# Decoder on one core: two gathered sums behind three quads, 28 of 64 sums moved into the second attention

## The chip, the cores and the metric

The kernel runs on one core of one Trainium2 chip, all in float32. The metric is the device time of one execution in microseconds (us). TensorE (PE) multiplies, VectorE (DVE) and ScalarE (ACT) work elementwise, GpSimd (POOL) issues the gathers and scatters, SyncE (SP) issues the plain transfers; 16 DMA engines carry them.

## What is computed

A decoder of two layers on x of 4 sequences by 1024 tokens by 256. After each block the residual is added and a layer norm taken:

```python
x = _layernorm(x + _L0_attn_ref(x, ...))    # retention, 8 heads
x = _layernorm(x + _L0_xattn_ref(x, ctx))   # 16 heads against 77 context rows
x = _layernorm(x + _L0_ffn_ref(x, ...))     # 64 experts, top 8 of them, and 2 shared experts
x = _layernorm(x + _L1_attn_ref(x, ...))    # linear attention with a memory
x = _layernorm(x + _L1_xattn_ref(x, ctx))
x = _layernorm(x + _L1_ffn_ref(x, ...))     # 8 gated experts, top 2
```

The change is in the third line and where it runs into the fourth. The first feed-forward is, for each token, `sum over its 8 experts of cw[e] * (silu(x @ W1[e] + B1[e]) @ W2[e] + B2[e])`, plus two shared experts of hidden width 512.

## The kernel before

The program has four phases, each a set of five instruction streams (one an engine): attention 1 (`attention_phase`, layer 0), the first feed-forward (`feed_phase`), attention 2 (the same function, layer 1) and the second feed-forward (`gated_phase`). A phase waits in `begin_here` for the last transfers of the one before. Tokens go in 8 steps of 4 x 128.

**Feed-forward.** Attention 1 has scattered each token's row into 8 places of a list in HBM (`lists`), sorted by expert in pages of 128 rows. The phase takes them in 80 quads of four pages. For quad n SyncE loads 512 KB (`load_quad`), TensorE transposes them (line 1680), multiplies them by the first weights (1692) and by the second (1703), ScalarE copies and applies silu (1551, 1575), and SyncE stores 512 KB to `results`. VectorE copies the weights of quad n+1 into place, four of the first kind (1597) and four of the second (1602), a quad ahead of TensorE. Between the quads lie the units of the shared experts (lines 110 and 127: 8 a step), the weights of the tokens, and the sums.

**Weights.** "weigh" jobs on VectorE, six a step, turn two tables of a step into the 8 weights of each token: compare, multiply, reduce (1648, 1652, 1654) for two pairs of sequences. SyncE loads the tables of a step into `routed` (`load_route`, 1493); only the compare and the multiply read them.

**Sums.** There are 64, one for each step s and eighth k (number n = 8s + k). For sum n GpSimd issues four gathers of 128 rows each from `results` (`gather`, line 1405), a small operation before them (`rest`, line 158), into one of four buffers; it needs the sum four numbers back to be done. VectorE adds the rows, times their weights, to the step's accumulator (`add_up`, line 1420, four instructions). Some gathers carry more work:
- k = 0 waits for the stores of all quads that can hold the step's rows (24 + 8s of them);
- k = 1 issues the accumulator's load (`load_base`, line 1387);
- k = 4 computes the scale of the norm of step s-1 (`scale`, lines 1375 and 1377), after that step's statistics;
- k = 7 issues the store of step s-1 (`store`, line 1381), and waits for its norm.

VectorE takes the statistics (1429, 1435) with sum k = 7 and the norm of step s-1 (`norm`, line 1441) behind sum k = 4 of step s. There are two accumulators.

**Where they lie.** `feed_order` writes out the order of the jobs: the first 24 quads have two units in three; from quad 24 on (`begun`) every other quad has a unit, and from quad 26 on each has one sum, as long as sums are left; those up to `LATE` - 1 (40 of 64) stay in the phase. Units end at quad 65. Each engine follows this order. GpSimd, which has only gathers here, issues `LATE + AHEAD` groups in a row.

**Late sums.** The other 24 are called from attention 2 by `late_on_pool` (gather of n + 3) and `late_on_vector` (sum n, and the norm if n % 8 is 4). Three stand ahead of its loop, behind `begin_here` and some memsets; 21 and the last norm hang on jobs of the loop, which `with_late` lists.

**Attention 2's order.** `SEQUENCE1` lists jobs with a lead; in loop step t a job with lead a works on step t - a of the tokens. Each engine takes its part of each job in this order. Of one loop step: wout and its norm (ln2 for the second norm), q (query), rank, four mx (maximum of the scores, line 830, GpSimd not involved), sig, tri, num, up (state), sc (scores, exponential on ScalarE, line 645), pv, wo, ln1 (the first norm), put (scatters, line 592). For ln1 and ln2 VectorE takes statistics, GpSimd computes the scale (lines 540 to 543) and ScalarE applies it (656 for ln1, 664 for ln2):

```python
    ("x1t", 2, 0), ("x1t", 2, 1), ("wout", 3, 0), ("wout", 3, 1), ("q", 2, 0), ("rank", 4, 0), ("q", 2, 1),
    ("ln2", 3, 0), ("put", 4, 0), ("lqk", 1, 0), ("mx", 2, 0), ("lv", 1, 0), ("sig", 1, 0), ("x2t", 3, 0),
    ...
    ("sc", 2, 2), ("ln1", 1, 0), ("pv", 2, 1), ("sc", 2, 3), ("pv", 2, 2), ("pv", 2, 3),
```

The waits that order late work on GpSimd against VectorE:

```python
            if s >= 1 and k == 7:
                store(pool, s - 1)
            ...
            if c >= NG:
                pool.wait_ge(summed, c - NG + 1)
```

## Time and profile before

| | |
|---|---|
| median of 3 runs | 2044.65 us (2043.0 to 2046.52) |
| the profiled execution | 2043.22 us, span 2041.2 us |
| TensorE busy | 1712.8 us (84%), mean granted clock 0.911 |
| VectorE busy | 1168.8 us (57%) |
| GpSimd busy | 922.9 us (45%) |
| ScalarE busy | 628.1 us (31%) |
| first feed-forward, quads | 640 to 1124 us |
| attention 2 | 1128 to 1600 us |
| second feed-forward | 1600 to 2041 us |

A row of a timeline gives start and duration in us, engine, line, operation, the output and inputs by their names, and in brackets how long the engine had been idle and what released it. `big` is one large buffer: the first weights, the gather buffers and the accumulators lie in it. In the windows a clock of 1.00 is TensorE's full speed, and the DMA share is the mean busy share of the 16 engines.

### The profile page before, as it was taken

The numbers are of one execution on the slowest core, as the hardware profiler recorded it, in microseconds if no ns is written. First come the engines' busy times: TensorE is split into PE (matmuls) and PEld (weight loads), VectorE is DVE, ScalarE is ACT, GpSimd is POOL, SyncE is SP. The second block draws the span as 40 slices with busy tenths as digits, with TensorE's granted clock in tenths as the row PEclk, the third lists the DMA queues.
The fourth block names the chain that finished last, engine by engine and source line by source line (L and its number), as shares of the span: only waits on it lengthen the run. The fifth ranks groups of instructions, "written<-read, shape, count | busy, mean of one in ns | idle before, by whom it ended". The sixth has DMA issues, their size and how long they took to land.

```text
span 2041.2 us, 49463 instructions
## 1 busy us (share of the span) xinstructions
PE 1712.8 (84%) x19787; PEld 1385.2 (68%) x19787; DVE 1168.8 (57%) x3042; ACT 628.1 (31%) x957; POOL 922.9 (45%) x1020
## 2 busy tenths in 40 slices
PE   3899999987859999777788449989997499999994
PEld 2677777776536776555566327777775399999993
DVE  3467777775302545667554537876765245665564
ACT  0233333332212555434446113434433011111110
POOL 0016777888850004888882576542322201222223
PEclk9999999998879999889989668878988699999997
DMA  9415665575693777878878633223101512333332
GB/s 307 154 36 182 203 205 180 180 256 187 180 247 104 230 218 250 265 251 260 259 253 280 226 91 96 72 70 135 44 33 37 180 48 71 94 93 92 98 96 62
DMA packets 269648, 322.85 MB, mean 158 GB/s; under 512 B 25083, under 2 KB 245487, under 8 KB 268655
## 3 DMA queue, kind: packets, MB, share of 16 engines
q1 hardware_dynamic: 236399, 227.38, 35.2%
q0 software_dynamic: 33024, 92.32, 14.1%
q8 instruction: 160, 2.62, 0.5%
q14 instruction: 65, 0.53, 0.1%
HBM read 157.22 MB, written 162.40 MB: 157 GB/s over the span
## 4 chain that ended last, share of the span: by engine, by line
PE 58%; POOL 14%; DVE 8%; DMA 6%; issue 6%; ACT 5%; SPq 2%; DVEq 0%; POOLq 0%; ACTq 0%
PE wide L2031 13%; POOL big L1405 7%; PE d_yp L2043 6%; ACT pt L645 3%; PE bank L994 3%; PE wide L1160 3%; PE wide L110 3%; PE wide L127 2%; POOL rest_ones L158 2%; PE bank L1175 2%; PE bank L1183 2%; PE wide L1163 2%; PE e_yp L1703 2%; PE wide L1147 2%; PE wide L1692 2%
## 5 line engine op out<-in xcount | busy, mean ns | idle before, releaser
L1405 POOL DMA_INDIRECT big<-results,slots x256 | 263.0, 1027 | 266.5 <-DMA results<-e_y 190.5
L2031 PE MATMUL wide<-d_xt,d_ws 128*128 128x128 f32 x2272 | 278.7, 277 | 0.6 <-issue 0.6
L2031 PEld LDWEIGHTS wide<-d_xt,d_ws 128*128 128x128 f32 x2272 | 272.3, 193 | 4.5 <-issue 1.0
L583 POOL DMA_INDIRECT lists<-big,slots x160 | 158.8, 993 | 82.3 <-issue 37.8
L645 ACT ACTIVATE pt<-wide 77x2048 f32<-77x2048 f32 x64 | 119.9, 1873 | 164.8 <-PE wide L1163 161.9
L1420 DVE SCALAR_TENSOR_TENSOR big<-big,weights 128x256 f32<-128x256 f32 x256 | 107.2, 480 | 83.5 <-DMA big<-results,slots 72.8
L1692 PE MATMUL wide<-e_xt,e_w1s 128*64 128x128 f32 x1280 | 96.1, 297 | 65.5 <-DVE e_w1s L1597 65.5
L127 PE MATMUL wide<-shared_sw,shared_sh 128*128 128x256 f32 x512 | 125.8, 390 | 25.6 <-DVE big L1661 25.6
L127 PEld LDWEIGHTS wide<-shared_sw,shared_sh 128*128 128x128 f32 x512 | 99.7, 196 | 69.0 <-DVE big L1661 29.4
L1900 POOL DMA_INDIRECT d_picked<-results,slots x64 | 63.5, 992 | 181.3 <-DMA results<-d_y 168.6
L1931 ACT ACTIVATE d_gate<-wide 128x512 f32<-128x512 f32 x71 | 42.4, 597 | 326.7 <-PE wide L2031 326.7
L2043 PE MATMUL d_yp<-d_wd,d_h 128*128 x568 | 134.2, 380 | 0.0
L158 POOL TENSOR_TENSOR rest_ones<-rest_ones 128x4 f32<-128x4 f32 x120 | 133.1, 1110 | 2.2
L110 PE MATMUL wide<-shared_sx,shared_sw 128*128 128x512 f32 x256 | 131.7, 639 | 2.5 <-ACT shared_sh L118 2.5
L837 DVE RECIPROCAL rden<-bank 128x256 f32<-128x256 f32 x64 | 112.1, 1751 | 37.6 <-PE bank L1175 36.5
L1692 PEld LDWEIGHTS wide<-e_xt,e_w1s 128*64 128x64 f32 x1280 | 75.1, 147 | 81.1 <-DVE e_w1s L1597 72.4
L2043 PEld LDWEIGHTS d_yp<-d_wd,d_h 128*128 128x128 f32 x568 | 102.8, 191 | 10.9
L540 POOL TENSOR_TENSOR rs<-mv,eps 128x4 f32<-128x4 f32 x32 | 6.6, 206 | 228.0 <-DVE mv L694 227.8
L1551 ACT ACTIVATE e_xt<-e_xp 128x1024 f32<-128x1024 f32 x80 | 81.9, 1024 | 83.5 <-PE e_xp L1680 83.5
L1962 DVE COPY d_ws<-big 128x1024 f32 x142 | 92.4, 693 | 26.4 <-issue 25.3
L1980 DVE TENSOR_TENSOR d_h<-d_gate,wide 128x512 f32<-128x512 f32 x71 | 48.7, 686 | 97.2 <-PE wide L2031 97.2
L1703 PE MATMUL e_yp<-e_w2s,e_ht 64*128 64x256 f32 x640 | 100.9, 438 | 1.5 <-ACT e_y L1551 1.5
(277 smaller groups left out, 3538.6 us busy)
## 6 DMA issues: line engine op xcount, KB each, us to landing
lists<-zero SPq DMA_DIRECT2D x20, 2048.0 KB, 14.3
e_x<-lists SPq DMA_DIRECT2D x80, 512.0 KB, 5.6
results<-e_y SPq DMA_DIRECT2D x80, 512.0 KB
d_x<-lists SPq DMA_DIRECT2D x71, 128.0 KB, 2.2
results<-d_y SPq DMA_DIRECT2D x71, 128.0 KB, 1.7
e_w<-in_L_w SPq DMA_DIRECT2D x2, 4096.0 KB, 38.9
x<-in_x SPq DMA_DIRECT2D x8, 512.0 KB, 5.0
shared_sw<-in_x_t SPq DMA_DIRECT2D x32, 128.0 KB
```

The lines of the kernel that those rows point to most:

```text
L110: ins = nc.tensor.matmul(sp_h, self.sw1[:, c, u * P:(u + 1) * P], self.sx[:, s % 2, c], start=c == 0, stop=c == KC - 1)
L127: ins = nc.tensor.matmul(sp_y[b // 2][:, b % 2 * DM:(b % 2 + 1) * DM], self.sh[:, n % 2, b * P:(b + 1) * P], self.sw2[:, u], start=u == 0 ...
L158: step(self.nc.gpsimd.tensor_tensor(self.ones[:, 1], self.ones[:, 0], self.ones[:, 0], ALU.pow))
L583: pool.indirect_dma_start(out=lists, out_offset=bass.IndirectOffsetOnAxis(ap=slots[:, b, i, k:k + 1], axis=0), in_=z2[i % 3][:, b, :], in_ ...
L645: empties(nc.scalar.activation(pt[0:CTX, p % 2].rearrange("k (j n) -> k j n", j=4), ps[0:CTX], ACT.Exp, scale=score_scale), job)
L837: step(nc.vector.reciprocal(rden[:, p % 2], ps[:, KC * P:]))
L1405: pool.indirect_dma_start(out=picked[:, c % NG, b, :], out_offset=None, in_=results[0:-(-PAGES_OF_STEP[s] // 4) * 4 * R0, :], in_offset=ba ...
L1420: ins = nc.vector.scalar_tensor_tensor(out=acc[s % NA][:, b], in0=picked[:, n % NG, b], scalar=weights[:, b, s, k:k + 1], in1=acc[s % NA][ ...
L1692: ins = mm(hp[h * H0:(h + 1) * H0, a * R0:(a + 1) * R0], w1s[:, j % NW1, h, a, c], xt[:, j % 2, h, a, c], start=c == 0, stop=c == KC - 1)
L1703: ins = mm(yp[:, h, a * DM:(a + 1) * DM], ht[lanes, j % 2, a], w2s[lanes, j % NW2, a, 0:DM], start=True, stop=True)
L2031: ins = mm(out[T % 2][:, a * P:(a + 1) * P], ws[:, T % NW, n, c, a * P:(a + 1) * P], xt[:, T % 2, c], start=c == 0, stop=c == KC - 1)
L2043: ins = mm(yp[T % 2][:, 0:DM], h[:, T % 2, c * P:(c + 1) * P], wd_flat[:, bass.ds(e * (HC * DM) + c * DM, DM)], start=c == 0, stop=c == HC ...
```

## The change

Sums lie behind two of three quads from quad 26 on, so that 36 fit by quad 79 (`LATE` goes from 40 to 36). The other 28 are late: three of them, gathers and sums, stand ahead of `begin_here` of attention 2 and its memsets, and 25 and the last norm hang on jobs of the loop, five instead of four in each of four loop steps (behind q, two mx, num and now up). With this each late number moves: the groups with k = 7 (47, 55, 63) were issued at sig 0, num 1 and num 3; now 47 is at wo 0, 55 at the last mx of loop step 3, and 63 at q of loop step 5, ahead of ln2. The load of a step's route tables is issued one job sooner, at the last weigh job of the step before.

```diff
--- before.py
+++ after.py
@@ -190,7 +190,7 @@
 
     behind = [("x0t", 0, 1), ("sig", 0, 0), ("tri", 0, 1), ("num", 0, 1), ("ct", 0, 0), ("wo", 0, 1)]
     for i in range(4):
-        behind += [("q", i, 1), ("mx", i, 1), ("mx", i, 3), ("num", i + 1, 1)]
+        behind += [("q", i, 1), ("mx", i, 1), ("mx", i, 3), ("num", i + 1, 1), ("up", i + 1, 0)]
     out = []
     for job in order:
         out.append(job)
@@ -543,6 +543,9 @@
                 nc.gpsimd.tensor_tensor(rs[:, which, 3], rs[:, which, 2], rs[:, which, 1], ALU.mult)\
                     .then_inc(rstd[which], 1)
 
+            if not first:
+                for n in range(LATE, LATE + 3):
+                    late_on_pool(pool, n)
             begin_here(pool)
             nc.gpsimd.memset(half[:], -0.5)
             nc.gpsimd.memset(minus[:], -1.0)
@@ -551,9 +554,6 @@
             if first:
                 nc.gpsimd.memset(zero[:], 0.0).then_inc(pool_ready, 1)
             pool.wait_ge(pool_ready, POOL_READY - (2 if first else 0))
-            if not first:
-                for n in range(LATE, LATE + 3):
-                    late_on_pool(pool, n)
             pool.wait_ge(consts, 16 * len(loads))
             if first:
                 for n in range(ES):
@@ -693,6 +693,9 @@
                 nc.vector.bn_aggr(mv[:, which, numbers[0]], stats[:, which, numbers[0]])
                 nc.vector.bn_aggr(mv[:, which, numbers[1]], stats[:, which, numbers[1]]).then_inc(mv_done[which], 1)
 
+            if not first:
+                for n in range(LATE, LATE + 3):
+                    late_on_vector(dve, n)
             begin_here(dve)
             if first:
                 nc.vector.memset(state[:], 0.0).then_inc(state_done, 1)
@@ -702,9 +705,6 @@
                 make(nc.vector.memset(v[:], 1.0))
             make(nc.vector.memset(vals[:], 0.0))
             make(nc.vector.memset(ones[:], 0.0))
-            if not first:
-                for n in range(LATE, LATE + 3):
-                    late_on_vector(dve, n)
             dve.wait_ge(consts, 16 * len(loads))
             make(nc.vector.tensor_reduce(mask2[:], head_mask[:].rearrange("p (m h) -> p h m", h=2), AX.X, ALU.add))
             make(nc.vector.tensor_reduce(sel_at[:], ident[:].rearrange("p (r n) -> p n r", r=4)[:, 0:4], AX.X, ALU.add))
@@ -1223,7 +1223,7 @@
 PAGES_OF_STEP = [(NB * P * K0 * (s + 1)) // R0 + E0 - 1 for s in range(STEPS)]
 
 
-LATE = STEPS * K0 - 24
+LATE = STEPS * K0 - 28
 AHEAD = 3
 FIRST_UNITS = 20
 PLAN_BEHIND = UNITS + 4
@@ -1274,7 +1274,7 @@
         else:
             weights(1)
             units(1 if j % 2 else 0)
-        if j >= begun + 2:
+        if j >= begun + 2 and (j - begun) % 3:
             sums(1)
     while unit[0] <= TOTAL:
         units(1)
@@ -1506,9 +1506,9 @@
                         load_quad(n + NX)
                     if n:
                         store_quad(n - 1)
-                if kind == "weigh" and n % 6 == 0 and n:
-                    sp.wait_ge(weighed, n - 1)
-                    load_route(n // 6)
+                if kind == "weigh" and n % 6 == 5 and n + 1 < 6 * STEPS:
+                    sp.wait_ge(weighed, n)
+                    load_route((n + 1) // 6)
                 if kind == "unit" and n and n % UNITS == 0 and shared < STEPS:
                     sp.wait_ge(experts.full, n)
                     experts.load_rows(sp, src_t, shared)
```

## Rows read from the trace of the kernel before

**Rows 1.** The page, part 4: the chain that ended last, shares of the span by engine

```profile
PE 58%; POOL 14%; DVE 8%; DMA 6%; issue 6%; ACT 5%; SPq 2%; DVEq 0%; POOLq 0%; ACTq 0%
```

**Rows 2.** Waits, 802 to 1127 us: engine line waited for, us, times, longest

```profile
DVE big L1420 <- DMA big<-results,slots: 68.7, 27, 4.6
...
PE wide L1692 <- DVE e_w1s L1597: 65.1, 21, 6.8
```

**Rows 3.** Line L1405, 788 to 1086 us: duration ns min/median/max, first and last start

```profile
L1405 POOL DMA_INDIRECT big<-results,slots x172: 942/967/2157, 788.4 to 1084.6; - x172
```

**Rows 4.** Timeline of VectorE, first feed-forward: start us, us, what, idle before

```profile
802.11 1.67 DVE L1420 SCALAR_TENSOR_TENSOR big<-big,weights 128x256 f32<-128x256 f32 x4 [5.30 <-DMA big<-mid]
...
875.70 1.22 DVE L1648 TENSOR_TENSOR big<-e_routed,e_slots_f 128x1024 f32<-128x1024 f32 x1 [4.90 <-DMA e_routed<-route]
...
1069.70 1.67 DVE L1420 SCALAR_TENSOR_TENSOR big<-big,weights 128x256 f32<-128x256 f32 x4 [1.37 <-DMA big<-results,slots]
```

**Rows 5.** Timeline of TensorE, first feed-forward

```profile
909.80 1.97 PE L1692 MATMUL wide<-e_xt,e_w1s 128*64 128x128 f32 x16 [6.49 <-DVE e_w1s L1597]
...
924.59 1.99 PE L110 MATMUL wide<-shared_sx,shared_sw 128*128 128x512 f32 x4
...
928.14 1.04 PE L1680 MATMUL e_xp<-e_ident,e_x 128*128 128x128 f32 x8
...
1095.44 1.09 PE L1680 MATMUL e_xp<-e_ident,e_x 128*128 128x128 f32 x8
...
1098.55 1.09 PE L1680 MATMUL e_xp<-e_ident,e_x 128*128 128x128 f32 x8
...
1118.41 1.09 PE L1692 MATMUL wide<-e_xt,e_w1s 128*64 128x128 f32 x16
```

**Rows 6.** Windows: us, busy us of PE, PEld, DVE, ACT, POOL, clock, DMA share, GB/s

```profile
640.00:788.00 148.00, 145.37 (x1040) 103.99 (x1039) 71.94 (x236) 80.59 (x121) 0.00 (x0) 0.98 0.69 217
...
802.00:1118.50 316.50, 248.44 (x1850) 179.06 (x1852) 196.46 (x660) 145.07 (x221) 233.20 (x222) 0.89 0.82 263
...
1085.00:1115.00 30.00, 26.18 (x268) 19.88 (x264) 13.72 (x69) 22.02 (x35) 0.60 (x1) 1.00 0.97 315
```

**Rows 7.** Timeline of GpSimd, end of the feed-forward and attention 2

```profile
1064.88 0.96 POOL L1405 DMA_INDIRECT big<-results,slots  x1 [0.30 <-issue]
...
1165.56 0.81 POOL L1381 DMA_DIRECT2D mid<-big  x1 [11.31 <-DVE big L1441]
...
1198.93 0.21 POOL L540 TENSOR_TENSOR rs<-mv,eps 128x4 f32<-128x4 f32 x1
...
1284.24 0.19 POOL L540 TENSOR_TENSOR rs<-mv,eps 128x4 f32<-128x4 f32 x1 [8.30 <-DVE mv L694]
...
1314.16 0.96 POOL L592 DMA_INDIRECT lists<-shared_sw,slots  x1 [0.30 <-issue]
...
1333.79 0.95 POOL L1405 DMA_INDIRECT big<-results,slots  x1 [0.30 <-issue]
...
1351.72 0.20 POOL L540 TENSOR_TENSOR rs<-mv,eps 128x4 f32<-128x4 f32 x1 [10.66 <-DVE mv L694]
```

**Rows 8.** Timeline of ScalarE, attention 2

```profile
1200.73 2.08 ACT L656 ACTIVATE x<-x,rs 128x256 f32<-128x256 f32 x4 [25.52 <-POOL rs L543]
...
1286.29 2.06 ACT L656 ACTIVATE x<-x,rs 128x256 f32<-128x256 f32 x4
...
1336.56 2.08 ACT L656 ACTIVATE x<-x,rs 128x256 f32<-128x256 f32 x4 [3.24 <-POOL rs L543]
```

**Rows 9.** Timeline of VectorE, attention 2

```profile
1142.88 0.16 DVE L709 TENSOR_REDUCE mask<-head_mask 128x2 f32<-128x8 f32 x1 [7.09 <-DMA memory<-in_L_norm]
...
1163.89 1.37 DVE L1441 TENSOR_SCALAR big<-big,sums_mv 128x256 f32<-128x256 f32 x4
...
1268.58 1.66 DVE L1420 SCALAR_TENSOR_TENSOR big<-big,weights 128x256 f32<-128x256 f32 x4
...
1355.82 1.67 DVE L1420 SCALAR_TENSOR_TENSOR big<-big,weights 128x256 f32<-128x256 f32 x4
```


## What it will do to the time

> **What bounds the kernel now.** I read the chain of waits first: its shares [rows 1] name TensorE 58% and GpSimd 14%, so somewhere GpSimd sets the pace. The waits of the first feed-forward say where: VectorE stands 68.7 us before its sums for gathered rows, and TensorE 65.1 us for staged expert weights [rows 2]. These are one wait seen twice. VectorE works in program order, so a sum that waits for its rows also holds back the weight copies written behind it. GpSimd itself never stops: 172 gather instructions between 788.4 and 1085.6 us [rows 3] are 43 groups of four, 6.91 us each, and each quad has one sum. So from the first sum (802.11) to the last (1069.70) [rows 4] 40 quads go at 6.9 us.
>
> TensorE would not need that. A quad alone takes 3.11 us (1095.44 to 1098.55) and a shared unit 3.55 (924.59 to 928.14) [rows 5]; with half a unit per quad that is 4.9 us. The last 14 quads have neither sum nor unit and are at the transfers' limit: 315 GB/s over 1085 to 1115 at a busy share of 0.97, while the whole stretch from 802 to 1118.5 moves 263 GB/s at 0.82 [rows 6].
>
> **Part 1: two sums behind three quads (feed-forward).** The condition drops every third sum, so 36 sums lie behind quads 26 to 79 instead of 40 behind 26 to 65. Three limits for this stretch, now 316.3 us (802.1 to 1118.4, the last inward group [rows 4, 5]):
> - GpSimd: 36 groups by 6.91 from 788.4 end at 1037; a sum starts 4.8 us after its last gather's issue (1064.88 [rows 7], 1069.70 [rows 4]) and takes 1.67: some 242 us after 802.
> - TensorE: 54 x 3.11 + 20 units x 3.55 = 239 us.
> - Transfers: 263 GB/s x 316.5 us = 83.2 MB now. Four gather groups (each four times 128 rows of 1 KB, 0.524 MB, as much as one quad's load) and one step's load and store go out of it, each as much again: 6 x 0.524 = 3.1 MB. 80.1 MB at 315 GB/s are 254 us.
>
> All three are close, so I don't take the largest as it stands. The plain quads behind 65 need 3.1 us of TensorE but about 4.7 of transfers (1.05 MB for load and store, 0.35 for gathers, 0.09 for the accumulators); the 40 before need 5.1 us of transfers against 4.9: 40 x 5.1 + 14 x 4.7 = 270, less some 6 us for loads and gathers that are ahead at the start, 264. Nothing overlaps fully; at 5% lost it is 277. **Term: -40 us**; bounds -62 (254 us reached) and -18 (298 us, each quad 0.8 us over the transfer time). I take the value nearer the transfers' row because with four buffers the gathers run ahead and VectorE stops meeting them.
>
> The Trainium skill ("DMA: Bandwidth & Descriptors", Specifications) states an HBM limit of about 358 GB/s per core. By it the bytes would need only 224 us, and the 242 us of GpSimd would bound; the stretch would shrink by over 60 us. No stretch of this length here shows more than 315.
>
> **Part 2: route rows a quad sooner.** SyncE issues the load at the sixth part of a step's weights, ahead of the next quad's waits. Its wait (five parts done) is the same number, and only the reduce, which doesn't read the rows, is still open. VectorE waited 4.90 us at 875.70 [rows 4]. Ahead of quad 24 TensorE is 98% busy regardless (145.4 of 148 us, [rows 6]); behind it the wait would eat part of term 1. I take 0 by itself; between 0 and -5. Behind SyncE's load nothing is queued that is late: one issue of half a microsecond.
>
> **Part 3: three late sums ahead of the wait for the quads.** Before, GpSimd waited for the last quad's store and issued three groups beside the constants' loads, which hide them. Now groups 39 to 41 go out while the last quads drain. What they bring lies ahead of attention 2's first norm. Now group 47, the last of a step's eight, must wait for VectorE's norm of the step before; GpSimd idles 11.31 us until 1165.56, then issues five groups, and the scale for the first norm starts at 1198.93 [rows 7]: ScalarE stands 25.52 us until 1200.73 [rows 8]. After the change groups 42 to 46 go out between 1143 (the constants' landing, at which VectorE goes on at 1142.88 [rows 9]) and about 1184: each needs the sum three late places back, and these come at 1156, 1164, 1167 and 1172, so GpSimd has three groups' work (19 us) behind 1164. Group 47 then needs the norm after "wo", about 1183: 1184 + 0.8 + 6.3 = 1191 instead of 1198.9. **Term: -7.5 us**; between -12 and 0. The transfers of these twelve gathers now share the drain with the last stores: 0 to +2, taken 0.
>
> **Part 4: 28 late sums instead of 24, five a step instead of four.** This is where the change costs. GpSimd has the gathers and the norms' scales in one queue. A group costs 6.27 us there: from the last scatter (ends 1315.12) to the last gather (ends 1334.74) are three groups and a store, 0.81 us by the one at 1165.56 [rows 7]. The groups that end a step (47, 55, 63) carry a store that waits for VectorE's norm, which is issued with the same late sum. By steps of the attention, all in today's clock:
> - Loop steps are counted from 0, as the schedule does. Step 2: the fifth group fits; GpSimd ends about when the scale's input is ready: +0.5.
> - Loop step 3: group 55 moves to the last maximum. The sum there starts at 1268.58 and takes 1.66, the norm 1.37 by the one at 1163.89 [rows 9]: 1271.6. Then store 0.8, a base load as long and three groups 18.8: 1292.1. The scale is issued at 1284.24 today with 8.30 us of idleness ahead [rows 7], and ScalarE takes it at 1286.29 without a wait [rows 8]: +7.9, and the exponential queued behind it on ScalarE, with its product on TensorE, are late by the same.
> - Loop step 4: behind the scatters (1315.12) come four groups (25.1) and a two-instruction scale, which I put at 1.2 since the four-instruction one takes 1.8 (1198.93 to 1200.73 [rows 7, 8]), where three groups and a store are now: 1341.4 against 1334.74, and ScalarE already waits 3.24 us today [rows 8]: +6.6.
> - Loop step 5: group 63 now stands ahead of the second norm's scale. VectorE's sum starts at 1355.82 [rows 9]; 1357.5 + 1.4 + 0.8 + 6.3 = 1366.0 against 1351.72 [rows 7]: 14 later. Between 0 and 4 us of it TensorE may have as slack, I allow 2: +12.
> - Four more sums on VectorE, 1.67 us each: 0 to +6.7, taken +2, since most fall where it waits for TensorE.
> - Two new idle stretches of 8 and 12 us. After 6.49 us of idleness a group of 16 matmuls took 1.97 us instead of 1.09 [rows 5], the pace of the lower of the two clock levels (1.2 against 2.4 GHz); the catch-up there cost some 3 us. 0 to +6, taken +3.
>
> **Term: 0.5 + 7.9 + 6.6 + 12 + 2 + 3 = +32 us**; bounds +10 (the waits overlap with slack I don't see) and +42.
>
> **Sum:** -40 + 0 - 7.5 + 32 = -15.5. The profiled execution took 2043.22 us with a span of 2041.2; it becomes about 2027.7. It stands 1.4 us below the median of the three runs (2044.65), within their spread, so I give **2028**.
>
> **Rivals.**
> (a) *Slower: the step-ending groups win.* Place: the GpSimd queue of the attention's loop steps 3 to 5. Price: +42 with both clock losses, no slack and all sums in full, against a feed-forward that gets only -27 as the transfers leave more gaps, and -7.5: 2043.2 + 7.5 = 2051. It decides from the point where part 4 costs more than parts 1 and 3 bring. For it: the queue order is certain. Against it: the feed-forward's wait is large and plain [rows 2].
> (b) *Much faster.* The feed-forward reaches its 254 us, -62, and the late groups cost only +20 as the scales find slack: 2043.2 - 62 - 7.5 + 20 = 1994; half-way, about 2008. For it: 315 GB/s is held for 30 us [rows 6]. Against it: only where nothing but quads ran. By the page's 358 GB/s it would be this case.
> (c) *The change doesn't reach its aim.* VectorE still meets each group because dense transfers lengthen the groups (6.91 us here against 6.27 in the attention [rows 3, 7]); at 8.3 us a group the stretch is 36 x 8.3 - 7 = 292 us and brings only -25, which part 4 less part 3 gives back: within 4 us of 2043.
>
> **How the numbers follow.** A measurement of this kernel can tell about 0.2%, 4 us, from no change. Forecast (2012 to 2038): 0.52. Rival (b), 1994 to 2012: 0.17. Rival (c), 2039 to 2047: 0.10. Rival (a), 2047 to 2060: 0.21. Faster is the forecast with (b), 0.69; same is (c), 0.10; slower is (a), 0.21. Eight in ten lie in 2003 to 2051: about half of (b) and half of (a) are left out. The forecast's own range is 2012 to 2038.
>
> **What would show it.** Right: between the first sum and the last quad some 277 us instead of 316; VectorE's wait for gathered rows under 20 us instead of 68.7, TensorE's for staged weights under 25; transfers there at about 0.9; GpSimd with idle time in the feed-forward; groups 39 to 41 ahead of the memsets; in the attention GpSimd's store standing for the norm three times, ScalarE waiting for the scale about 8 us at loop step 3 and 10 at step 4, and some 14 at step 5's second norm. Wrong: a wait for rows still in front of each sum (rival c), quads held by their own loads for over 0.8 us each (rival a), or ScalarE's waits missing (rival b).

## The result, and the profile after

| | before | after |
|---|---|---|
| median, us | 2043.83 (2040.63 to 2046.52, 4 runs) | 2010.65 (2002.87 to 2014.55, 4 runs) |
| ratio, 95% interval | | 0.9835 [0.9812, 0.9857] |
| profiled execution, its span, us | 2043.22, 2041.2 | 2002.87, 2000.9 |
| first feed-forward, first sum to last inward group, us | 316.3 | 250.5 |
| attention 2, loop steps 3, 4, 5, us | 45.2, 52.8, 47.6 | 55.4, 59.4, 60.0 |

The change brought 33 us; the forecast was 16. The profiled execution is the fastest of its four and shows 40; two later profiles of the same kernel have 252.9 and 254.5 us in the feed-forward. In three of the five series of experiments below (first, third and fifth) the kernel before took 2219 to 2229 us instead of 2044, at a mean granted clock of about 0.87 instead of 0.91, once on the very chip that gave 2044 in another series, so ratios and stretches are compared within a series.

The 40 us divide so: 7.1 less ahead of the first sum (3.2 of it before the feed-forward begins, where nothing was changed), 65.8 less from there to the last inward group, 1.0 less from there to ScalarE's first scale in attention 2, 0.4 less to the first output product, 33.8 more from there to the last group of output products, and 0.2 more behind it.

The chain of waits, shares by engine (answers to [rows 1]):

```profile
PE 65%; POOL 8%; DVE 8%; DMA 6%; ACT 5%; issue 5%; SPq 2%; DVEq 0%; POOLq 0%; ACTq 0%
```

GpSimd's share fell from 14 to 8%, TensorE's rose from 58 to 65. The waits between 795 and 1046 us (answers to [rows 2]; us in total, times, longest):

```profile
DVE e_w1s L1597 <- PE wide L1692: 24.2, 13, 4.5
PEld e_xp L1680 <- DMA e_x<-lists: 17.8, 12, 4.1
DVE big L1648 <- DMA e_routed<-route: 17.0, 3, 7.7
...
PE e_xp L1680 <- DMA e_x<-lists: 13.3, 8, 3.7
```

The two waits of [rows 2] are all but gone: VectorE waits 0.3 us for gathered rows (68.7 before), TensorE 7.2 us for staged weights (65.1 before). VectorE now waits for TensorE to free a weight buffer, and TensorE for its own quads' loads. The windows of the stretch, whole, up to the last shared unit, and behind it (columns as in [rows 6]):

```profile
794.98:1045.48 250.50, 230.06 (x1856) 168.28 (x1854) 182.79 (x628) 146.09 (x221) 205.62 (x187) 0.97 0.95 313
794.98:985.00 190.02, 178.41 (x1369) 128.82 (x1368) 141.16 (x466) 107.45 (x162) 158.00 (x142) 0.98 0.93 305
985.00:1045.48 60.48, 51.65 (x490) 39.47 (x488) 41.63 (x162) 38.63 (x59) 47.62 (x46) 0.94 1.01 340
```

The same windows with only the products with the first weights (line 1692, 16 a quad) count the quads, first of this kernel, then of the kernel before over its whole stretch:

```profile
794.98:985.00 190.02, 40.02 (x576) 31.17 (x576) 0.98 0.93 305
985.00:1045.40 60.40, 17.40 (x240) 13.62 (x240) 0.94 1.01 340
...
802.11:1118.35 316.24, 63.17 (x816) 49.41 (x816) 0.89 0.82 263
```

They are 36 and 15, together 51 quads in either kernel. TensorE is busy 178 of the first 190 us. The last 60 us move 340 GB/s, more than the 315 that was taken for the limit [rows 6]. The shared units on TensorE show the pace:

```profile
868.79 1.98 PE L110 MATMUL wide<-shared_sx,shared_sw 128*128 128x512 f32 x4
878.51 1.98 PE L110 MATMUL wide<-shared_sx,shared_sw 128*128 128x512 f32 x4
888.23 1.98 PE L110 MATMUL wide<-shared_sx,shared_sw 128*128 128x512 f32 x4
897.94 1.98 PE L110 MATMUL wide<-shared_sx,shared_sw 128*128 128x512 f32 x4
907.66 1.98 PE L110 MATMUL wide<-shared_sx,shared_sw 128*128 128x512 f32 x4
921.12 3.10 PE L110 MATMUL wide<-shared_sx,shared_sw 128*128 128x512 f32 x4
```

They come 9.72 us apart, within 0.1 of two quads (3.11 each) and a unit (3.55) of [rows 5]: there TensorE runs at its own limit, up to a stumble of 3.7 us ahead of the unit at 921.12, in which it waited 3.14 us for a staged weight. Of the 18 spans between units from 791.16 to 981.31, 12 have these 9.72 us; the other six (10.3 to 15.1) cost 15 us, by waits for staged weights and for the quads' own loads. Attention 2, ScalarE (answers to [rows 8]) and then GpSimd (answers to [rows 7]):

```profile
1126.82 2.08 ACT L656 ACTIVATE x<-x,rs 128x256 f32<-128x256 f32 x4 [23.52 <-POOL rs L543]
1166.72 2.06 ACT L656 ACTIVATE x<-x,rs 128x256 f32<-128x256 f32 x4
...
1219.83 2.07 ACT L656 ACTIVATE x<-x,rs 128x256 f32<-128x256 f32 x4 [8.16 <-POOL rs L543]
```

```profile
1197.51 0.82 POOL L1381 DMA_DIRECT2D mid<-big  x1 [9.88 <-DVE big L1441]
1218.04 0.21 POOL L540 TENSOR_TENSOR rs<-mv,eps 128x4 f32<-128x4 f32 x1
...
1302.26 0.86 POOL L1381 DMA_DIRECT2D mid<-big  x1 [18.49 <-DVE big L1441]
1309.29 0.21 POOL L540 TENSOR_TENSOR rs<-mv,eps 128x4 f32<-128x4 f32 x1
```

The store that ends a step (L1381) stands 9.88 and 18.49 us for VectorE's norm with the scales' input ready behind it; ScalarE waits 8.16 us at loop step 3 where it waited for nothing, 6.67 us at step 4 instead of 3.24, and 14.12 us before step 5's second norm. That is the loss as forecast.

### The profile page after: what moved, and what is told of

Read it like the earlier page. It is cut to its first block, busy times and chain, and to the rows that moved or that the text cites. A ratio compares the mean times of both kernels' runs of the same rounds, so it can differ in the third digit from the quotient of the medians.

```text
span 2000.9 us, 49465 instructions
## 1 busy us (share of the span) xinstructions
PE 1701.5 (85%) x19787; PEld 1379.9 (69%) x19787; DVE 1166.0 (58%) x3042; ACT 628.3 (31%) x957; POOL 928.6 (46%) x1020
## 4 chain that ended last, share of the span: by engine, by line
PE 65%; POOL 8%; DVE 8%; DMA 6%; ACT 5%; issue 5%; SPq 2%; DVEq 0%; POOLq 0%; ACTq 0%
PE wide L2031 13%; PE d_yp L2043 6%; POOL big L1405 5%; PE wide L110 4%; PE wide L127 4%; ACT pt L645 3%; PE bank L994 3%; PE wide L1160 3%; PE e_yp L1703 3%; PE bank L1175 3%; PE wide L1692 3%; PE e_xp L1680 3%; PE wide L1147 3%; PE bank L1183 2%; PE wide L1163 2%
## 5 line engine op out<-in xcount | busy, mean ns | idle before, releaser
L1405 POOL DMA_INDIRECT big<-results,slots x256 | 268.7, 1050 | 264.1 <-DMA results<-e_y 187.8
L1980 DVE TENSOR_TENSOR d_h<-d_gate,wide 128x512 f32<-128x512 f32 x71 | 48.7, 686 | 96.7 <-PE wide L2031 96.7
L1597 DVE COPY e_w1s<-big 128x128 f32 x320 | 53.0, 236 | 85.7 <-PE wide L1692 69.8
L1680 PE MATMUL e_xp<-e_ident,e_x 128*128 128x128 f32 x640 | 87.3, 280 | 16.1 <-DMA e_x<-lists 14.8
L1680 PEld LDWEIGHTS e_xp<-e_ident,e_x 128*128 128x128 f32 x640 | 73.0, 143 | 35.0 <-DMA e_x<-lists 20.0
```

Of the source, the lines that this page charges most:

```text
L1405: pool.indirect_dma_start(out=picked[:, c % NG, b, :], out_offset=None, in_=results[0:-(-PAGES_OF_STEP[s] // 4) * 4 * R0, :], in_offset=ba ...
L1680: ins = tr(xp[:, h, (a * KC + c) * P:(a * KC + c + 1) * P], x[:, j % NX, h, a, c * P:(c + 1) * P], ident[:])
```

## The experiments

"Stretch" is the time from the first sum to the last inward group.

### First series (kernel before 2229.45 us)

**One sum behind each quad**, the rest as in the change:

```
-        if j >= begun + 2 and (j - begun) % 3:
+        if j >= begun + 2:
```

> The change with one part undone: each quad from 26 on has one sum again, so the 36 sums lie behind quads 26 to 61 and 18 quads have none. Theory (the spread pays): GpSimd's 6.9 us a group sets the first 36 quads again, 36 x 6.9 = 248 us, then 18 quads at 3.4 us, 61 us: about 310 us from the first sum to the last inward group instead of 250, and the kernel is about 2010 + 58 = 2065 us or more, slower than before by some 20 us, since the late sums keep their price. Rival (the gain comes from the four sums that left the phase, at 6.9 us each, and from what stands ahead of the second attention): the stretch stays below 290 us and the time below 2030.

Ratio 1.007 [1.0041, 1.0098], stretch 306.5 us at 264 GB/s: the theory, against the rival's 290.

**Without the sooner route rows:**

```
-                if kind == "weigh" and n % 6 == 5 and n + 1 < 6 * STEPS:
-                    sp.wait_ge(weighed, n)
-                    load_route((n + 1) // 6)
+                if kind == "weigh" and n % 6 == 0 and n:
+                    sp.wait_ge(weighed, n - 1)
+                    load_route(n // 6)
```

> The change without the sooner route rows. Theory (they only take a wait of VectorE that TensorE does not feel, or felt by 1 or 2 us in four of the steps): 0 to +6 us against the change. Rival (the 4 us that the quads before the first sum are shorter, and more behind it, are theirs): +8 us or more, with VectorE's wait for the tables back in front of quads and TensorE waiting for staged weights after it.

Ratio 1.0022 [0.9992, 1.0053], stretch 285.5 us, loop steps 3 to 5 together 192.0 us.

**The three late sums back behind the wait for the quads**, on GpSimd and VectorE alike:

```
-            if not first:
-                for n in range(LATE, LATE + 3):
-                    late_on_pool(pool, n)
             begin_here(pool)
...
             pool.wait_ge(pool_ready, POOL_READY - (2 if first else 0))
+            if not first:
+                for n in range(LATE, LATE + 3):
+                    late_on_pool(pool, n)
```

> The change with the three late sums behind the wait for the last quads and the memsets again, as before; numbers 36 to 38, and the marks in the loop are those of the change. Theory (the groups are merely moved under a cover that already was there; their rows compete with the last stores and constants): the stretch from the last inward group to the first keys product falls from 28.4 to about 25 us, but GpSimd issues groups 39 to 41 some 20 us later and the first norm of the second attention comes about as late as the queue is full: 0 to +8 us in all. Rival (the place ahead is what brings the first norm sooner): +12 us or more, ScalarE's wait for the first scale back above 20 us.

Ratio 0.9935 [0.9908, 0.9962], stretch 268.8 us, 26.3 us from there to the keys, 51.6 to ScalarE's first scale.

**VectorE's norm of a step one late sum sooner:**

```
-                if eighth[0] >= K0 and eighth[0] % K0 == 4:
+                if eighth[0] >= K0 and eighth[0] % K0 == 3:
...
-            if n < STEPS * K0 and n % K0 == 4:
+            if n < STEPS * K0 and n % K0 == 3:
```

> The change with VectorE's norm of a step behind the fourth sum of the next (k = 3) instead of the fifth, in both phases, so that the group with k = 7 finds it done one late place sooner. Theory (GpSimd's store waits for the norm in the same late place: 9.9 us of idleness in loop step 3, 18.5 in step 5, and ScalarE late by it): the waits go, loop step 3 is about 8 us shorter, step 5 about 12, the first norm 2 to 5; step 4 stays, as it is filled by scatters and groups. Together -15 to -25 us against the change, about 1990 us. Rival (the queue's length, five groups a step, is the cost and not the store's wait): within 5 us of the change.

Ratio 0.9831 [0.9746, 0.9916], stretch 275.1 us, loop steps 3 to 5 together 172.5 us against 192.0 in the second experiment. What follows: without the thinner sums the gain of the feed-forward is gone (306.5 against 268.8 to 285.5) while the late sums' cost stays, hence slower than before. The route rows are not worth nothing: the stretch without them is 10 to 17 us longer than the two with them. This series lacks the unedited change, against which three of the expectations are written, so they can't be judged by it; the second and fourth series have it.

### Second series (kernel before 2043.46 us)

**The change again.**

> The change itself, unedited, as the control of this series. In its first profile the stretch from the first sum to the last inward group took 250.5 us and the three loop steps 3 to 5 of attention 2 together 174.8 us (145.6 before). In the series of the four experiments before this one the attention ran at a granted clock of about 0.78 and the whole kernel took 2229 us instead of 2044. Theory 1 (the gain of the feed-forward doesn't depend on that, the loss of the attention does not either): ratio to the kernel before 0.983 on either kind of chip. Theory 2 (where TensorE has the lower clock its work covers less of the feed-forward's gain): ratio 0.983 at a clock of 0.91, about 0.99 at 0.86.

2009.24 us, ratio 0.9847 [0.9806, 0.9887], stretch 252.9 us, loop steps 55.6, 60.8, 60.0 us.

**24 late sums, 40 sums behind three of four quads:**

```
-LATE = STEPS * K0 - 28
+LATE = STEPS * K0 - 24
...
-        if j >= begun + 2 and (j - begun) % 3:
+        if j >= begun + 2 and (j - begun) % 4:
...
-        behind += [("q", i, 1), ("mx", i, 1), ("mx", i, 3), ("num", i + 1, 1), ("up", i + 1, 0)]
+        behind += [("q", i, 1), ("mx", i, 1), ("mx", i, 3), ("num", i + 1, 1)]
```

> 24 late sums as before the change, and 40 sums behind three of four quads; the other two parts as in the change. Theory 1 (GpSimd's pace, 6.96 us a group, sets the feed-forward; the late sums cost 29 us in loop steps 3 to 5): four groups more make the stretch 40 x 6.96 = 278 us, 28 longer than with the change, and the three loop steps go back from 174.8 to about 146 us; the sum is within 5 us of the change, 2006 to 2016 where the kernel before takes 2044 (ratio 0.981 to 0.986). Theory 2 (the transfers set the stretch, at 318 GB/s): four groups are 2.1 MB, 7 us, and the loss in the attention goes: about 20 us faster than the change, ratio 0.974.

1998.8 us, ratio 0.9774 [0.9734, 0.9814], stretch 273.0 us, loop steps 45.2, 52.8, 48.7 us. The waits of its stretch:

```profile
DVE big L1420 <- DMA big<-results,slots: 37.9, 14, 5.3
...
PE wide L1692 <- DVE e_w1s L1597: 22.0, 12, 4.6
```

With 40 groups VectorE meets them again: four groups cost 20 us against the control, less than the 28 of theory 1 and far more than the 7 of theory 2. The attention gives back 30. So with the norm where the change has it, four late sums cost more there than in the feed-forward.

**The kernel before with the sooner route rows alone** (the second edit above, the other way round):

> The kernel before with the sooner route rows alone. Theory 1 (the wait for the route rows lay under GpSimd's pace of one group a quad, so it is worth nothing until that pace falls): ratio 0.998 to 1.001, and the stretch from the first sum to the last inward group stays within 4 us of 316. Theory 2 (each of the route waits held TensorE too): 4 waits of 4 us, ratio 0.990 to 0.993. Of the change without this part the stretch took 285.5 us where it took 268.8 and 275.1 with it in the same series, so theory 1 expects the gain to appear only together with the other part.

2039.02 us, ratio 0.9981 [0.9966, 0.9997], stretch 317.2 us. Theory 1: alone it is worth 0.2%, about what can be told from nothing, and the stretch is as long as before. What it gives lies ahead of the stretch: from TensorE's first transposes of the phase to the first sum 151.7 us instead of 157.6.

**One more small operation on GpSimd ahead of each group in the feed-forward:**

```
                 shared_sems.rest(pool)
+                if c < LATE + AHEAD:
+                    shared_sems.rest(pool)
```

> The change with one more of the small operations ahead of each group of gathers in the first feed-forward, which moves no byte (the one there takes 1.25 us with the wait behind it). Theory 1 (GpSimd's instruction stream alone sets the stretch): 36 x 1.3 to 1.5 us, the stretch goes from 250.5 to 297 to 305 us, the kernel 47 to 54 us slower than the change, ratio to the kernel before 1.006 to 1.012. Theory 2 (transfers or TensorE set it, and GpSimd had room): the stretch grows by less than 20 us, ratio under 0.994.

2036.05 us, ratio 0.997 [0.9951, 0.9989], stretch 271.8 us:

```profile
790.18:1062.02 271.84, 238.33 (x1857) 174.18 (x1855) 183.19 (x625) 146.83 (x222) 227.38 (x218) 0.94 0.89 290
```

By the stretch, 19 us over the control for some 43 us of work (36 operations, about 1.2 each), theory 2 held by a hair; by the ratio (27 us over the control) neither did. The rest of the 27 lies behind the stretch: from the last inward group to ScalarE's first scale 87.1 us against the control's 76.8. GpSimd took in about half of what was added and passed the rest on: it had room in the change, but little, and stands just behind TensorE.

### Third series (kernel before 2221.31 us)

**The norm sooner, again** (fourth experiment's edit):

> The change with VectorE's norm of a step one late sum sooner (behind the fourth sum of the next step instead of the fifth), so that the group that ends a step doesn't wait for it. In the slower series it took the loop steps 3 to 5 of attention 2 from 192 us (without it) to 172.5. Theory 1 (in attention 2 the step-ending group, which waits for the norm with the scales' inputs queued behind it, is what the late sums cost): from the control's 176.4 us for the three steps (55.6, 60.8, 60.0) to 152 to 160, the kernel 16 to 24 us faster than the change, ratio to the kernel before 0.973 to 0.977. Theory 2 (the mere number of groups, five of 6.3 us a step, sets the steps): less than 6 us gained, ratio 0.980 to 0.984. The feed-forward stays at 250 to 254 us in both.

Ratio 0.9796 [0.9752, 0.9839], stretch 274.8 us, the three loop steps 168.1 us (189.8 in the twelfth experiment, whose norm is as in the change). The 21.7 us less are theory 1's size; its 152 to 160 us and its ratio were written for the series at 2044 us and don't hold here.

**Three of four quads with the norm sooner** (both edits):

> 24 late sums behind three of four quads, as in the sixth experiment (0.9774, feed-forward 273.0 us, loop steps 3 to 5 146.7 us), with the norm one sum sooner. Theory 1 (the sooner norm pays only where a step's groups don't fit): 0 to 5 us gained over the sixth experiment, ratio 0.975 to 0.978, so that it and 28 late sums with the sooner norm come within 0.3% of each other. Theory 2 (the wait for the norm costs wherever it stands, the first norm of the attention too, 25.3 us of waiting on ScalarE there): 8 us or more, ratio under 0.974.

Ratio 0.9773 [0.9734, 0.9812], stretch 273.8 us; within 0.3% of the ninth, as theory 1 had it, but the intervals are too wide here to tell the two apart.

**The change with 6.8 MB more of stores.** `store_more` issues one 512 KB transfer on SyncE's queue:

```
                     if n:
                         store_quad(n - 1)
+                    if n >= 28 and n % 4 == 0:
+                        store_more((n - 28) // 4)
```

> The change with 13 more stores of 512 KB in the first feed-forward, behind every fourth quad from 28 to 76, from a tile that stays as it is to memory of their own: 6.8 MB more on the queue of SyncE, nothing more on TensorE, VectorE or GpSimd. The control moves 313 GB/s over the stretch at a share of 0.95. Theory 1 (the transfers set the whole stretch at that rate): 6.8 MB / 0.313 = +22 us, stretch 272 to 277 us, ratio 0.993 to 0.996. Theory 2 (TensorE sets it behind the first 40 quads, a shared unit each 9.72 us, which is two quads of 3.11 and a unit of 3.5, and the transfers only the last 14 quads, which get 4 of the 13 stores): the shared units keep their 9.72 us for the most part, +6 to +12 us, stretch 258 to 265 us, ratio 0.986 to 0.990.

Ratio 0.9954 [0.9932, 0.9976], stretch 280.3 us at 308 GB/s. The fifth series runs this kernel again.

**Without the sooner route rows, again:**

> The change without its sooner route rows. On the slower chip its stretch took 285.5 us where two kernels with them took 268.8 and 275.1. Theory 1 (at the new pace the waits for the route rows stand in TensorE's path): four waits of 3 to 5 us more, the stretch grows from 252.9 to 262 to 270 us, ratio 0.989 to 0.993. Theory 2 (what was forecast: nothing by itself): stretch within 4 us of 252.9, ratio 0.983 to 0.986.

Ratio 0.9987 [0.9958, 1.0015], stretch 285.1 us. This series too has no unedited change in it: against the ninth kernel, whose feed-forward is the change's but for the norm, the route rows are worth 10 us of stretch, as in the first series, and the added bytes 5.

### Fourth series (kernel before 2044.65 us)

**The change, as control:**

> The change itself, unedited, beside the next three on the same chip. On a chip as the first: ratio 0.983 to 0.985, feed-forward stretch 250 to 253 us, loop steps 3 to 5 of attention 2 together 175 to 177 us. On a chip as that of the first and third series (kernel before 2221 to 2229 us): stretch 268 to 276 us as in the runs there with the same feed-forward, loop steps 185 to 193 us; by the theory that the lower clock hides part of the gain, ratio 0.986 to 0.994; by the theory that it doesn't, 0.983.

2008.16 us, ratio 0.983 [0.9803, 0.9856], stretch 254.5 us, loop steps 55.4, 60.7, 60.0 us. No series where the kernel before took 2219 us or more has the unedited change, so what it is worth there stays open.

**Without the sooner route rows:**

> The change without its sooner route rows. Theory 1 (at the new pace the waits for the route rows lie in TensorE's path, and GpSimd then waits for the norm that VectorE has behind them): 10 to 17 us more in the feed-forward than the control, ratio to the kernel before 0.006 to 0.008 above the control's. Theory 2 (nothing by itself, as forecast): within 0.002 of the control.

2020.94 us, ratio 0.988 [0.9853, 0.9907], stretch 268.7 us. The route rows on VectorE, first of this kernel, then of the control:

```profile
826.00 1.23 DVE L1648 TENSOR_TENSOR big<-e_routed,e_slots_f 128x1024 f32<-128x1024 f32 x1 [8.23 <-DMA e_routed<-route]
...
865.89 1.23 DVE L1648 TENSOR_TENSOR big<-e_routed,e_slots_f 128x1024 f32<-128x1024 f32 x1 [14.23 <-DMA e_routed<-route]
...
904.09 1.22 DVE L1648 TENSOR_TENSOR big<-e_routed,e_slots_f 128x1024 f32<-128x1024 f32 x1 [9.10 <-DMA e_routed<-route]
```

```profile
818.50 1.23 DVE L1648 TENSOR_TENSOR big<-e_routed,e_slots_f 128x1024 f32<-128x1024 f32 x1 [4.49 <-DMA e_routed<-route]
...
853.90 1.22 DVE L1648 TENSOR_TENSOR big<-e_routed,e_slots_f 128x1024 f32<-128x1024 f32 x1 [10.51 <-DMA e_routed<-route]
...
885.37 1.23 DVE L1648 TENSOR_TENSOR big<-e_routed,e_slots_f 128x1024 f32<-128x1024 f32 x1 [5.00 <-DMA e_routed<-route]
```

The same three waits are each about 4 us longer without the sooner load, a quad's time. TensorE and GpSimd stand behind VectorE and pay for it, TensorE for staged weights and GpSimd for the norm (wait of TensorE, then GpSimd's timeline):

```profile
PE wide L1692 <- DVE e_w1s L1597: 21.1, 5, 8.8
```

```profile
912.79 0.95 POOL L1381 DMA_DIRECT2D mid<-big  x1 [14.35 <-DVE big L1441]
```

TensorE's 21.1 us in 5 waits are 7.9 us in 3 in the control. Theory 1, at 0.005 instead of 0.006 to 0.008: 14.2 us of the stretch, 12.8 of the median. Ahead of the first sum too the quads take 155.4 us here and 153.1 in the control.

**The norm sooner:**

> The change with the norm of a step one late sum sooner. Theory 1 (the wait for the norm is what the fifth group costs): loop steps 3 to 5 together 16 to 24 us below the control, ratio 0.008 to 0.012 below the control's. On the slower chip this kernel had 0.9831 and 0.9796. Theory 2 (the number of groups sets the steps): less than 6 us and 0.003 below the control.

1982.75 us, ratio 0.9704 [0.9672, 0.9735], stretch 254.0 us, the fastest of all kernels here. TensorE's output products (L1183) of this kernel, and then of the control:

```profile
1175.19 3.62 PE L1183 MATMUL bank<-wout,att_t 128*128 128x256 f32 x16
1221.07 3.62 PE L1183 MATMUL bank<-wout,att_t 128*128 128x256 f32 x16
1280.21 5.18 PE L1183 MATMUL bank<-wout,att_t 128*128 128x256 f32 x16
1328.75 1.46 PE L1183 MATMUL bank<-wout,att_t 128*128 128x256 f32 x6
```

```profile
1176.90 3.69 PE L1183 MATMUL bank<-wout,att_t 128*128 128x256 f32 x16
1232.32 4.98 PE L1183 MATMUL bank<-wout,att_t 128*128 128x256 f32 x16
1293.01 3.66 PE L1183 MATMUL bank<-wout,att_t 128*128 128x256 f32 x16
1353.00 2.32 PE L1183 MATMUL bank<-wout,att_t 128*128 128x256 f32 x10
```

Loop steps 45.9, 59.1 and 48.5 us against 55.4, 60.7 and 60.0: steps 3 and 5 are back within a microsecond of before with five groups in each. Theory 1 there, at a ratio 0.0126 below the control's, just over the 0.008 to 0.012 expected; step 4, where four groups lie behind the scatters, keeps its length (52.8 us in the kernels with one group less a step), so there it is the number of groups. GpSimd's store waits 2.83 us and not at all:

```profile
1191.91 0.82 POOL L1381 DMA_DIRECT2D mid<-big  x1 [2.83 <-DVE big L1441]
...
1275.33 0.86 POOL L1381 DMA_DIRECT2D mid<-big  x1
```

**Three of four quads with the norm sooner:**

> 24 late sums behind three of four quads, with the norm one sum sooner; 0.9773 on the slower chip, where the sixth experiment (0.9774, without the sooner norm, on a chip as the first) was not run. Theory 1 (the sooner norm pays only where a step's groups don't fit): 0.975 to 0.978, with 28 late sums and the sooner norm within 0.003 of it. Theory 2 (it pays at each step): under 0.974.

1994.92 us, ratio 0.9752 [0.9724, 0.978], stretch 270.2 us, loop steps 45.2, 52.8, 48.6 us. Theory 1 on the sooner norm: nothing in the steps, whose groups fit. Its second half fell: 28 late sums with the sooner norm are not equal but 12 us ahead.

### Fifth series (kernel before 2219.04 us)

**The 6.8 MB more, again:**

> The change with 13 more stores of 512 KB behind every fourth quad from 28 to 76, as in the eleventh experiment (on the slower chip the stretch took 280 us where the kernels with the same sums took 275). The control moves 313 GB/s over a stretch of 250.5 to 254.5 us. Theory 1 (the transfers set the whole stretch): 6.8 MB / 0.313 = +22 us, stretch 272 to 277 us, ratio 0.993 to 0.996. Theory 2 (TensorE sets it behind the first 40 quads, 9.72 us for two quads and a shared unit, and the transfers the last 14): +5 to +12 us, stretch 256 to 266 us, ratio 0.985 to 0.989, and the mean rate rises above 320 GB/s.

Ratio 0.9954 [0.9928, 0.9981], stretch 274.1 us:

```profile
933.33:1207.47 274.14, 237.32 (x1868) 173.52 (x1866) 186.19 (x632) 144.07 (x223) 208.27 (x195) 0.96 0.95 315
```

The bytes went into a stretch of the length that two kernels had without them (275.1 and 274.8, at 293 GB/s, both with the sooner norm); the same kernel took 280.3 in the third series, so a stretch is good to some 6 us from series to series. Theory 1's 272 to 277 us and its ratio came out as stated, but from a stretch that was as long before: of its 22 us at most 6 came, so the transfers did not set the whole stretch there. Where the kernel before takes 2044 us and the change moves 313 GB/s already, this wasn't measured; that the transfers pace the last 15 quads is read from TensorE's waits for its loads alone.

**The three late sums behind the quads, again:**

> The change with the first three late sums back behind the wait for the quads' last stores, beside the constants' loads; all else as in the change. Theory 1 (as forecast: the three groups ahead bring the first norm of attention 2 sooner, 7.5 us, of which 3.7 went to a later landing of the constants): from the keys' first product to the first scale on ScalarE 56 to 59 us instead of 52.4 (control), the stretch between last inward group and keys 24.5 to 26 instead of 27.1 to 28.4, the kernel 2 to 6 us slower than the change, ratio 0.984 to 0.987. Theory 2 (the three groups ahead take transfers and GpSimd's time from the last quads, and are worth nothing or less): stretch to the last inward group 3 us or more shorter, ratio 0.980 to 0.983.

Ratio 0.99 [0.9859, 0.994], stretch 267.8 us, 27.0 us from there to the keys, 51.9 to ScalarE's first scale. The stretch is 6 to 7 us shorter than with the sums ahead (268.8 and 267.8 against 275.1 and 274.8, though those have the sooner norm as well), and the first scale comes 2 to 4 us later (51.6 and 51.9 us against 49.8 and 48.1). Kernels of the same series with the norm as in the change have 48.5 us (second experiment) and 48.4 (seventeenth) to the first scale, and 29 us instead of 26.3 and 27.0 to the keys: the two nearly cancel, 77.6 us from the last inward group to the first scale in both, against 77.9 and 78.9 with the part undone. From the last inward group to the eighth output product the undone kernels take 5 and 9 us longer, in a spread of 10 between like kernels. By the stretch that is theory 2, by the ratio neither. A control beside it is missing, and where the kernel before takes 2044 us it wasn't tried: that the part is worth little either way is as much as the runs say.

## Why the prediction was right and wrong

**Part 1, -40 forecast, and the step that failed.** "40 x 5.1 + 14 x 4.7 = 270", less 6, and "at 5% lost it is 277" failed; the measured stretch is 250.5 us (252.9 and 254.5 in the later profiles). The mechanism held: with one sum behind each quad the stretch stays at 306.5 us, thinned out it falls. What was mis-sized is first the count. From the first sum to the last inward group TensorE takes 51 quads, not 54, and did so before the change: at the first sum VectorE has already staged quad 27. In the forecast's own form (36 x 5.1 + 15 x 4.7 - 6) x 1.05 is 260.5, 16 us less than 277. Second, the pace of the quads behind the last unit: 60.4 us for 15, 4.0 each, where 4.7 and the 5% make 4.9. The transfer rate under it, 315 GB/s, was no limit: they move 340 over those 60 us, and the densest part of them shows

```profile
992.86:1042.37 49.51, 40.68 (x386) 30.89 (x384) 37.69 (x145) 30.76 (x47) 38.57 (x35) 0.93 1.03 352
```

In the 30 us of [rows 6] TensorE took several quads at its own 3.11 us [rows 5], so the queues weren't asked for more all the time. The 36 quads before took 190.0 us, 5.3 each, which is the forecast's 5.1 with 5%. But they aren't held by the transfers at that pace: TensorE's own time is 36 x 3.11 + 18 x 3.55 = 176 us, and the rest are the six longer spans. So the value there is right by luck. The Trainium skill's 358 GB/s ("DMA: Bandwidth & Descriptors", Specifications), which I set aside, lies above every rate measured here over 50 us or more. The shrinking "by over 60 us" that I had derived from it came (62 to 66), though not by its sum: GpSimd's 36 groups took 7.2 us each and not 6.91, which makes its limit 254 us instead of 242. That is as long as the stretch itself, yet VectorE waited only 0.3 us for rows in it; so GpSimd did not set the stretch, but it had next to nothing to spare. The first half of rival (b) came true.

**Part 2, 0 forecast, between 0 and -5.** Also wrong, in its bound. In the stretch it is worth nothing alone (317.2 us against 316.3), but together with the thinner sums 14.2 us of stretch and 12.8 of the median. I had written that the wait "would eat part of term 1" and gave that part no number. Ahead of the first sum it isn't nothing either, though TensorE is "98% busy regardless": VectorE's four waits for the rows shrink from about 7.9 us to 4.2 to 5.2, and the time from TensorE's first transposes to the first sum from 157.6 us to 151.7 (alone) and 153.6 (in the change). Without the route rows the rest of the change brings about 24 us of the median (2020.94 against 2044.65), 8 more than the forecast's 16. Its stretch is 268.7 us, 8 below 277 and 8 above the 260.5 of the right count: by the right count the waits for the rows would have shown as gain that is missing, and the wrong one hid them. VectorE's waits for the rows did not go away in the stretch (17.0 us in 3; 9.5 in 3 before, where GpSimd's pace came first).

**Part 3, -7.5 forecast.** Two thirds of it came: from keys to first scale 57.6 us before, 52.9 after. But from the last inward group to the keys' product went 24.7 to 28.4 us: the constants land later beside the gathers. I allowed 0 to +2 and took 0. The two together went from 82.3 us to 81.3 (76.8 and 79.5 in the later profiles). In the two series where it was undone, the stretch was 6 to 7 us shorter as well. The net is nearer 0 than -7.5, and no run with a control beside it settles it.

**Part 4, +32 forecast, right.** Loop steps 3 to 5 took +10.2, +6.6 and +12.4 us where 7.9, 6.6 and 12 stood, 29.2 together. Counted from the first output product to the last group of them, +33.8 (324.5 to 358.3); the 4.6 us over match the 5.5 taken for step 2, VectorE's sums and the clock, which no run takes apart. The fifteenth experiment confirms the mechanism: with the norm one sum sooner, steps 3 and 5 lose their waits.

**Signs.** VectorE's wait under 20 us came (0.3 us for gathered rows), the two long stands of GpSimd's store (a third is 3.3 us), and ScalarE's 8 and 14 us; the 10 us at step 4 were 6.7. "GpSimd with idle time" did not come. The trace puts next to no idle time there, yet GpSimd took in about half of what the eighth experiment added: its gathers got shorter, 137.6 us in all where the control has 151.2, for 137 and 140 of them in the traces (over 1.3 us in 4 of 143 of them, in 18 of 144 in the first profile of the change), and its store's 4.1 us of waiting went. So its busy time is no measure of its room where the queues are this full.

## What to carry to other kernels

When a change removes the largest wait, work out anew every wait that lay under it: one that cost 4 us before (the route rows) was worth 13 behind it. Count the items between two marks in the trace itself and not from the order of the jobs: three quads too many made 16 us of the forecast. A rate read over 30 us in which an engine partly paces the transfers is no ceiling: 315 GB/s there, 340 later. Two errors of a sum can hide each other, so hold each term against the trace and not only the total. An instruction that waits for another engine, put ahead of others in a queue, costs as its wait and not as its length: issuing the norm one sum sooner was worth 25 us, with nothing added or taken away.

## What was unexpected of the hardware

Mixed loads, stores and gathers moved 340 GB/s over 60 us at a busy share of 1.01, and 352 at 1.03 over the densest 50, where quads without gathers had moved 315 at 0.97 over 30 us: the share is close to full in all three, and the rate differs by up to 12%. And a single gather on GpSimd is no constant: median 0.97 us, up to 2.23 in the change, so a group of four is 6.2 us at best and 7.2 on average there, with the scales, loads and stores between.
